# Token rows loaded at the end of the attention block, and turned copies ahead of roundings, in a two-layer vision tower on one core

## What is computed

```
h = h + attention(layernorm(h))          # windows of 32 tokens, 32 of them an image; softmax(q k / 4) v, then W_proj
flat = layernorm(h).reshape(8192, 128)
top_vals, top_idx = top_k(flat @ Wr, 2)  # 2 of 8 experts for each token
top_w = softmax(top_vals)
for e in range(8):
    hdn = gelu(flat @ W1[e] + b1[e]);  y = hdn @ W2[e] + b2[e]
    out = out + gate[:, e] * y           # gate is top_w where e was chosen, else 0
h = h + out
```

## Time and profile before

| | us |
|---|---|
| median of the runs | 1414.62 |
| runs | 1414.47, 1414.62, 1420.9 |
| the profiled execution | 1414.32 |
| its span in the profile | 1412.5 |
| layer 1's attention block, about | 848 to 1096 |
| token experts, about | 1096 to 1376 |
| adding the results, to the end | 1376 to 1412.5 |

### The profile page before, as it was taken

One profiled execution on the slowest core, in us unless ns is written; L12 is line 12 of the kernel. 1 busy time (PEld: TensorE's weight loads), 2 busy tenths in 40 slices (PEclk: granted clock), 3 DMA queues, 4 the chain that ended last, 5 costly groups with the idle time before them and its releaser, 6 DMA issues. The chain is left out here.

```text
span 1412.5 us, 26983 instructions
## 1 busy us (share of the span) xinstructions
PE 1181.6 (84%) x9386; PEld 794.1 (56%) x9386; DVE 934.5 (66%) x2612; ACT 994.4 (70%) x1348; POOL 561.7 (40%) x546
## 2 busy tenths in 40 slices
PE   3599999999999999979989987787861799999940
PEld 2344444444444444447768865676761688888830
DVE  4366868686868686669878873777651466666625
ACT  0498888888888888769768975445420799999930
POOL 3413333343434343211110010377776177677660
PEclk9799999999999999889999997788865899999975
DMA  3664737373737374232113100011116377777619
GB/s 86 119 177 99 178 98 180 96 182 94 187 89 187 86 191 104 76 131 77 60 60 120 61 0 1 17 46 46 47 46 232 119 238 240 236 248 246 231 28 354
DMA packets 93164, 180.58 MB, mean 128 GB/s; under 512 B 15597, under 2 KB 64200, under 8 KB 84960
## 3 DMA queue, kind: packets, MB, share of 16 engines
q1 hardware_dynamic: 72832, 129.18, 32.3%
q0 software_dynamic: 17344, 42.68, 9.3%
q10 hardware_dynamic: 2848, 6.95, 1.7%
HBM read 116.96 MB, written 63.12 MB: 127 GB/s over the span
## 5 line engine op out<-in xcount | busy, mean ns | idle before, releaser
L741 ACT ACTIVATE a_probs<-a_psS 128x1024 f32<-128x1024 f32 x512 | 483.1, 1034 | 83.1 <-PE a_psS L826 51.8
L838 PE MATMUL a_psO<-a_probs,a_v 128*32 128x256 f32 x4096 | 277.5, 389 | 17.7 <-DVE a_o_t L1015 17.4
L1252 DVE TENSOR_TENSOR f_g_lo<-f_g,f_g_hi 128x512 fp32r<-128x512 f32 x284 | 195.2, 689 | 116.7 <-ACT f_g L1159 115.4
L2043 POOL DMA_INDIRECT result<-f_out,f_idx x156 | 180.6, 1158 | 101.4 <-issue 57.6
L838 PEld LDWEIGHTS a_psO<-a_probs,a_v 128*32 128x32 f32 x4096 | 107.5, 110 | 151.6 <-issue 85.1
L1630 POOL DMA_INDIRECT queue<-all_row,all_idx x128 | 125.8, 983 | 38.6 <-issue 37.6
L826 PE MATMUL a_psS<-ag_qs,ag_ks 50*128 50x512 f32 x512 | 95.8, 450 | 12.8 <-DMA ag_qs<-a_gparts 5.9
L826 PE MATMUL a_psS<-a_qs,a_ks 50*128 50x512 f32 x512 | 96.4, 452 | 8.8 <-issue 4.6
L402 POOL TENSOR_TENSOR ag_rs_f<-ag_veps_f,all_half 128x4 f32<-128x4 f32 x32 | 33.9, 1058 | 124.7 <-DVE ag_veps_f L99 124.7
L1422 POOL TENSOR_TENSOR ah_rs<-ah_veps,all_half 128x4 f32<-128x4 f32 x16 | 18.5, 1154 | 154.3 <-DVE ah_veps L1435 154.2
L826 PEld LDWEIGHTS a_psS<-ag_qs,ag_ks 50*128 50x128 f32 x512 | 39.3, 188 | 59.6 <-ACT a_probs L741 30.2
(11 more groups left out here) (368 smaller groups left out, 2879.7 us busy)
## 6 DMA issues: line engine op xcount, KB each, us to landing
all_w<-experts SPq DMA_DIRECT2D x19, 1026.5 KB, 5.4
experts<-a_split POOLq DMA_DIRECT2D x32, 512.0 KB, 5.0
ag_qs<-experts SPq DMA_DIRECT2D x14, 1026.5 KB, 5.5
ag_ks<-experts SPq DMA_DIRECT2D x14, 1026.5 KB, 5.2
f_rows<-queue SPq DMA_DIRECT2D x39, 260.0 KB
f_w<-experts SPq DMA_DIRECT2D x8, 1026.5 KB, 5.4
qparts<-a_parts SPq DMA_DIRECT2D x16, 512.0 KB, 4.3
kparts<-a_parts SPq DMA_DIRECT2D x14, 512.0 KB, 3.2
```

The source lines that it names most:

```text
L741: nc.scalar.activation(probs[u % NPR][:, :], psS[score_buffer(u)][:, :, :].rearrange("p a n -> p (a n)"), ACT.Exp).then_inc(exp_done, 1)
L838: last = nc.tensor.matmul(psO[32 * g:32 * g + 32, a * HALF:(a + 1) * HALF], v[par][:, 2 * hp + p, kt, :], probs[u % NPR][:, cols:cols + HA ...
L1252: nc.vector.tensor_tensor(g_lo[i][:, n, :], g[:, n, :], g_hi[i][:, n, :].bitcast(F32), ALU.subtract).then_inc(lo_done, 1)
L2043: pool.indirect_dma_start(result, bass.IndirectOffsetOnAxis(ap=idx[i][:, j:j + 1], axis=0), out[i][:, j, :], None, bounds_check=2 * B * S ...
```

## The change

In block_attention the sync engine writes the last pad block (behind all experts' parts of the queue) at the start of the block, before its wait for the counts. After the plan it loads the parts of two tiles, not four, reads the first rows of two tiles into registers, waits for the pads and for all sends, and loads the rows of tiles 0 and 1. POOL's wait for the sends at the end of the block goes. The two row buffers and their semaphores are made in tower, outside both blocks, so that they don't share memory with the attention. token_experts loads no rows for tiles 0 and 1 and no longer begins with the rows of four tiles; from tile 2 on it loads a tile's rows and then its parts. In ScalarE's order the two copies copy_z now stand ahead of the drain and the two roundings first_bits.

```diff
@@ block_attention, sync engine
+            sp.dma_start(queue[E * STRIDE:E * STRIDE + CH, :].rearrange("(p i) c -> p i c", p=P), pad[:, :, :]).then_inc(padded, 16)
             sp.wait_ge(n_done, 1)
-            for e in range(E + 1):
-                first = e * STRIDE if e == E else e * STRIDE + sp.value_load(n_i[0:1, e:e + 1], min_val=0, max_val=B * S)
+            for e in range(E):
+                first = e * STRIDE + sp.value_load(n_i[0:1, e:e + 1], min_val=0, max_val=B * S)
                 sp.dma_start(queue[bass.ds(first, CH), :].rearrange("(p i) c -> p i c", p=P), pad[:, :, :]).then_inc(padded, 16)
             sp.wait_ge(planned, 1)
-            for i in range(len(w1)):
+            for i in range(len(rows)):
                 e = sp.value_load(tile_e[0:1, i:i + 1], min_val=0, max_val=E - 1)
                 sp.dma_start(w1[i][:, :], parts[bass.ds(e, 1), :, :].rearrange("o p c -> p (o c)")).then_inc(w1_in[i], 16)
+            starts = [sp.value_load(tile_row[0:1, i:i + 1], min_val=0, max_val=E * STRIDE) for i in range(len(rows))]
             sp.wait_ge(padded, 16 * (E + 1))
+            for p in range(NROW):
+                sp.wait_ge(sent[p], len(range(p, B, NROW)) * 16 * K * T)
+            for i in range(len(rows)):
+                sp.dma_start(rows[i][:, :, :], queue[bass.ds(starts[i], CH), :].rearrange("(p i) c -> p i c", p=P)).then_inc(rows_in[i], 16)
@@ block_attention, POOL
             send(B - 1)
-            for p in range(NROW):
-                pool.wait_ge(sent[p], len(range(p, B, NROW)) * 16 * K * T)
@@ block_attention, ScalarE
                 if b + 1 < B:
                     places(b + 1, 1)
+                if b:
+                    for ch in range(CPB):
+                        copy_z(b - 1, ch)
+                if b + 1 < B:
                     act.drain()
                     for ch in range(CPB):
                         first_bits(b + 1, ch)
-                if b:
-                    for ch in range(CPB):
-                        copy_z(b - 1, ch)
@@ token_experts, sync engine
             def load_rows(m):
                 first = sp.value_load(tile_row[0:1, m:m + 1], min_val=0, max_val=E * (B * S + CH))
-                if m >= 2:
-                    sp.wait_ge(meta_done, m - 1)
-                    sp.wait_ge(x_ps, m - 1)
+                sp.wait_ge(meta_done, m - 1)
+                sp.wait_ge(x_ps, m - 1)
...
-            for m in range(NW):
-                load_rows(m)
-            for m in range(NW, N):
+            for m in range(2, N):
                 load_rows(m)
                 load_parts(m)
@@ tower
+        rows = [c.sb(f"rows{i}", [P, TPC, ROW]) for i in range(2)]
+        rows_in = [c.sem(f"rows_in{i}") for i in range(2)]
```

More of the change, by code:

```diff
@@ L1546, in sequence_experts, with block_attention @@
                      x_ps, t_ps, t_read, y_done, NB, D, Rest(nc, shared, ahead, H, mean1, rstd1, score1, freed, t_read))
-def block_attention(nc, H, queue, counts, row, idx, sent, tile_e, tile_row, parts, w1, w1_in, ident, half, ahead, ins, B, S, D):
+def block_attention(nc, H, queue, counts, row, idx, sent, rows, rows_in, tile_e, tile_row, parts, w1, w1_in, ident, half, ahead, ins, B, S, D):
     SB = 32
@@ L1993, in _, with token_experts @@
             plan()
-def token_experts(nc, queue, result, tile_e, tile_row, ident, parts, w, w_in, B, S, D):
+def token_experts(nc, queue, result, rows, rows_in, tile_e, tile_row, ident, parts, w, w_in, B, S, D):
     E, _, WIDE = parts.shape
@@ L2006, in token_experts @@
         c = Core(nc, ctx, "f1")
-        rows = [c.sb(f"rows{i}", [P, TPC, ROW]) for i in range(2)]
         meta = [c.sb(f"meta{i}", [P, TPC, 2]) for i in range(5)]
@@ L2011, in token_experts @@
         x_ps, t_ps, t_read, y_done, meta_done, out_ready = (c.sem(n) for n in "x_ps t_ps t_read y_done meta_done out_ready".split())
-        rows_in, sent = ([c.sem(f"{n}{i}") for i in range(2)] for n in ("rows_in", "sent"))
+        sent = [c.sem(f"sent{i}") for i in range(2)]
         block = ctx.enter_context(nc.Block())
@@ L2151, in tower @@
             sent = [c2.sem(f"sent{p}") for p in range(3)]
-            block_attention(nc, H, queue, counts, row, idx, sent, tile_e, tile_row, experts[1], w1, w1_in, ident, half, ahead, ins, B, S, D)
-        token_experts(nc, queue, result, tile_e, tile_row, ident, experts[1], w1, w1_in, B, S, D)
+            block_attention(nc, H, queue, counts, row, idx, sent, rows, rows_in, tile_e, tile_row, experts[1], w1, w1_in, ident, half, ahead, ins, B, S, D)
+        token_experts(nc, queue, result, rows, rows_in, tile_e, tile_row, ident, experts[1], w1, w1_in, B, S, D)
         add_results(nc, H, result, out, B, S, D)
```

## The result

The changed kernel takes 1406.93 us (median of 15 runs, 1400.04 to 1412.15). The kernel before, run beside it on the same chip, takes 1420.22 (15 runs, 1406.94 to 1430.2), 5.6 more than the median of the three runs shown at first. The ratio is 0.9915, with a 95% interval of 0.9895 to 0.9934: faster by 0.66 to 1.05%. Two later rounds of the same kernel gave 0.9904 (0.9868 to 0.9941) and 0.9916 (0.9882 to 0.9949).

The account below looks back on a forecast made before the run. It took TensorE in token_experts as the bound, its start set by Pool's sends, attention's chain and the block's end. 1414.32 less 6.3 (copies) and 6.8 (boundary) gave 1401.2, forecast 1401.3 us; own range 1399 to 1403.5, wide 1397.5 to 1407.5.

Parts of the forecast that it names:

- Sum: Whole kernel: 1414.32 us of the profiled execution less 6.3 and 6.8 gives 1401.2, forecast as 1401.3.
- The copies: Attention batches 1 to 6: zT ahead of x_hi starts the router's logits 1.06 us earlier each; 6.3 us saved.
- the gap that Pool has between two instructions anyway is 0.3: Pool's six waits for the variance in attention: 8.2 us less 6 x 0.3 leaves 6.4 us of slack.
- The boundary: From the last send's issue (t) to token_experts' first transposition: t + 5.3 instead of t + 12.13; 6.8 us saved.
- Pool's drain of 2.68 from the last landing: End of the attention block: the drain, counted from the last send's landing, ends 5.0 us after that send's issue.
- the bound of the short drain: Attention block's end: the row landing, 5.1 us after the last send's issue, decides; 7.0 us saved.
- What comes behind: In token_experts: the later loads of parts 2 and 3 and of rows 3 are taken to cost 0.
- B: Attention block's end: a long Pool drain or late send landing replaces the old wait; saves 3.2, 1404.8 us; chance 0.17.
- C: Attention batches: shorter idleness ahead of the logits keeps the granted clock up; saves 9.2, 1398.3 us; chance 0.12.
- D: Attention: x_lo late, copies bring nothing (1407.5 us); or block's end: rows land no earlier (1408.0); chance 0.11.
- E: Attention batches: the swap puts a second lower-clock stretch on project, output and values; 7.2 us slower, 1421.5; chance 0.04.

Follow-up runs that it names:

- four parts ahead: The changed kernel with four expert parts instead of two loaded ahead of the rows; 8.15 us from the last send's issue to TensorE's first transposition.
- the copies alone: The kernel before with only the two zT copies moved ahead of the two x_hi roundings; ratio 0.9936, median 1410.35 us.
- the two runs of one half each: The kernel before with only ScalarE's swap, ratio 0.9936; the changed kernel with ScalarE's old order, ratio 0.9958.

## Why the prediction was right and wrong

**Sum: the step that failed.** It set 1401.3 (its own terms give 1401.2) by taking the changes off the 1414.32 of one execution, and leaned on the median of the runs being 0.3 away. That median was of three runs, which themselves reached 1420.9, and the range had no term for it. Over 30 runs before stands at 1419.22, from 1411.2 to 1428.2. With that base the same terms give 1419.2 - 13.1 = 1406.1, and the three medians of after are 1406.93, 1405.48 and 1406.25. Those 5 us have nothing to do with the change. Between the two profiled executions of before, the difference arises in layer 0's attention, whose last exponential starts 233 us ahead of the changed block, and follows the granted clock; and of the 30 runs the five fastest (1411 to 1414 us) show a mean granted clock of 0.914 to 0.918, the five slowest (1424 to 1428) 0.905 to 0.912. The execution that the forecast was built on had 0.917. The range's 10 us were made of the change's uncertainty alone; single executions of before spread over 17 in those 30 runs.

**The copies.** Forecast 6.3, measured 7.0 (239.1 to 232.1) in after and 7.6 alone. The mechanism is the one described: zT where x_hi was, TensorE's gap shorter by 1.3 (forecast 1.06), x_lo waiting for nothing, Pool's waits down from 8.2 to 1.7. The term mis-sized is "the gap that Pool has between two instructions anyway is 0.3": between a send and a root it can vanish from the rows altogether, as in 980.38 and 1002.92 above. So there was more slack than 6.4 to give up; 6.5 of the 8.2 went. The first of the six batches, which Pool doesn't bound, gained 0.7 (24.09 us from root to root, 23.39 after) where 1.06 was taken; the other five gained 1.1 to 1.4 each. That Pool caps the gain is borne out by the added Pool work. The gain also goes with the clock: with four parts ahead, two batches took 23.73 and 23.94 us from root to root, as long as before, with TensorE's gap at 2.0 and 1.9 all the same. The granted clock there was 0.78 and 0.79, and Pool waited 1.25 and 1.97 ahead of the roots.

**The boundary.** Forecast t + 5.3 and 6.8; measured 5.36 to 5.43, and 6.8. The parts, as the experiments separate them: last send landed at t + 2.31 (2.3 taken), rows out at t + 2.58 (2.5), first landing 2.74 later (2.6), and the crowd of four parts 3.3 when taken away alone (3.4). One step was right in its result and wrong in its reason. I counted Pool's drain of 2.68 from the last landing, which would be 1091.94 + 2.68 = 1094.6; it ended at 1093.3. Nor does it count from the last send's end: with four parts ahead that end is at 1085.99, and 2.68 later is 1088.7, but Pool's drain ended at 1091.6 (1071.9 + 19.66), just as the sync queue, behind the issue of the rows, came to the end of its own:

```profile
L1569 POOLq DRAIN  x1: 19660/19660/19660, 1071.9 to 1071.9; - x1
L1569 SPq DRAIN  x1: 122/122/122, 1091.4 to 1091.4; - x1
```

In after the two end together as well, at 1093.3 and 1093.2, and so in all seven executions in which Pool did not wait for its sends. So the block's end followed the sync queue there; why Pool's drain waits, no run shows. What decided was the landing of the rows, which the prediction named only as the bound of the short drain.

**What comes behind.** Part 2 went out 2.43 us after TensorE's start (2.5 forecast), landed 6.11 later, and was first used 15.76 after the start: covered by 7.2. PE to end is not longer but 0.5 shorter (312.8 to 312.2, 312.3 and 312.7). None of that is of the moved loads: the last expert product starts 256.0 to 256.1 us after the first transposition in both executions of before and all three of after. The difference lies behind it, where executions vary anyway (57.0 us in the copies alone, 56.8 in before, 56.1 to 56.6 in after).

**The rivals.** B fell: the sends land in 2.3 and the drain ends early. C fell: with the gap at 2.0 us instead of 3.3 the granted clock still falls in every batch, from root to root 0.92 at best and 0.86 on average. The rule of the Trainium skill beside C ("TensorE: Matmul & The Clock Gate", section "HAM oscillation — how this bites in real kernels") isn't refuted by this, since a gap was left; a kernel without one was not run. D fell by the two runs of one half each. E fell for the time, though not wholly in kind: one batch of after is at 0.77 and two of the run with four parts at 0.78 and 0.79, but none of the three takes longer than before.

## What to carry to other kernels

When a forecast is a difference, give it as one, and build its base and its range on the spread of executions, not on how near a profile lies to a median of three. A queue's own idle rows tell how much an engine off the path can give up, and adding work to that engine shows when it has become the pace. At a block's end look at what crowds the last transfer and at which engine waits for it: here two loads of 1 MB each, first used 28 us after the last send, and a block's end between a landing and the load behind it cost 3.3 and 4.0 us.

## What was not expected of the hardware

Two executions of one kernel, before, differ by 7.5 us when the second attention starts. The cause seen is TensorE's granted clock within layer 0's attention, where TensorE is busy over 90% of the time: 569.9 us at a mean of 0.96, 559.2 at 0.99. One fall to the lower level for 3.4 us costs about 1.4 us in the 64 exponentials around it.

Pool's drain took 2.676 us in each of five executions in which Pool had first waited for its sends, though all had landed. Where Pool did not wait itself, the drain began 13 to 14 us ahead of the last send and ended as the sync queue came to the block's end, 1.3 to 1.4 us after that queue had seen the last landing.
